# Last LayerNorm and output store moved into the block of the last experts, with the statistics taken on transposed sums

## The reference

```python
def _layernorm(x, axis=-1, eps=1e-05):
    m = jnp.mean(x, axis=axis, keepdims=True)
    v = jnp.var(x, axis=axis, keepdims=True)
    return (x - m) / jnp.sqrt(v + eps)

# ... seven such lines before it
x = _layernorm(x + _L3_ffn_ref(x, ...), axis=-1)     # L3_ffn: 8 routed experts (top 2) and a shared one
return x                                              # (4, 512, 128), float32
```

## Time and profile before

| | us |
|---|---|
| median of 3 runs | 1772.24 (1771.27 to 1776.8) |
| the profiled execution, own time | 1770.54 |
| its span, first to last instruction | 1768.4 |
| PE busy in it | 1613.3 (91%) |
| DVE / ACT / POOL busy | 1049.9 / 1012.7 / 746.8 |

### The profile page before, as it was taken

How to read it: one execution, slowest core, us unless ns; L and a number is a source line. 1 busy time by engine, 2 the same in 40 slices (tenths; PEclk the granted TensorE clock), 3 DMA queues, 4 the chain that set the end, 5 groups by cost and what they waited for, 6 DMA issues and landing times. The chain is left out here.

```text
span 1768.4 us, 28482 instructions
## 1 busy us (share of the span) xinstructions
PE 1613.3 (91%) x9207; PEld 1084.4 (61%) x9225; DVE 1049.9 (59%) x2605; ACT 1012.7 (57%) x2188; POOL 746.8 (42%) x683
## 2 busy tenths in 40 slices
PE   5888998888798899999799999999999999888998
PEld 3556754346596677777555555555458886344786
DVE  5865775623122666666366666666558886662675
ACT  4534563553243555555466666666548887754786
POOL 1234533105252566655265555555234443021463
PEclk8999998998899999999999999999989999989999
DMA  1008323000214223232211111111046562000420
GB/s 43 2 15 179 69 73 142 1 1 30 68 34 138 60 65 68 61 69 51 78 44 47 47 40 47 47 39 49 19 144 218 219 221 87 1 1 22 148 108 25
DMA packets 61868, 124.71 MB, mean 71 GB/s; under 512 B 14258, under 2 KB 29477, under 8 KB 55228
## 3 DMA queue, kind: packets, MB, share of 16 engines
q1 hardware_dynamic: 59580, 119.24, 23.1%
q0 software_dynamic: 2144, 3.70, 0.7%
HBM read 79.05 MB, written 11.02 MB: 51 GB/s over the span
## 5 line engine op out<-in xcount | busy, mean ns | idle before, releaser
L1992 ACT ACTIVATE h_probs<-psum,h_nmax 128x512 f32<-128x512 f32 (+3 forms) x256 | 133.2, 526 | 119.0 <-DVE h_nmax L2073 64.1
L2073 DVE CUSTOM_DVE_ANT_0 psum<-psum,h_mask 128x512 f32<-128x512 f32 (+3 forms) x256 | 122.6, 511 | 83.3 <-PE psum L1876 80.4
L917 ACT ACTIVATE psum<-psum,f_b 128x512 f32<-128x512 f32 x200 | 132.3, 662 | 30.0 <-PE psum L874 30.0
L1804 POOL TENSOR_TENSOR h_swapped<-h_swapped,rope_tables 128x512 f32<-128x512 f32 x64 | 81.8, 1278 | 153.6 <-DMA h_swapped<-h_raw 153.6
L840 POOL TENSOR_TENSOR e_lo<-e_gated,e_hi 128x512 fp32r<-128x512 f32 x59 | 76.0, 1289 | 150.3 <-ACT e_hi L929 150.3
L2425 ACT ACTIVATE a_probs<-psum,a_nmax 128x512 f32<-128x512 f32 (+3 forms) x128 | 67.5, 527 | 120.7 <-DVE a_nmax L2500 70.3
L2246 POOL TENSOR_TENSOR a_swapped<-a_swapped,a2f_a_tables 128x512 f32<-128x512 f32 x64 | 82.0, 1281 | 127.1 <-DMA a_swapped<-a_raw 127.0
L952 DVE TENSOR_TENSOR e_lo<-psum,e_hi 128x512 fp32r<-128x512 f32 x168 | 114.8, 683 | 24.9 <-ACT psum L917 24.9
L126 PE MATMUL psum<-rope_tables,mean_w 128*128 128x256 f32 x482 | 118.3, 396 | 7.0 <-ACT h_raw L1982 2.8
L1883 PEld LDWEIGHTS psum<-ident,h_probs 128*128 128x128 f32 x640 | 71.4, 141 | 80.4 <-issue 52.8
L1883 PE MATMUL psum<-ident,h_probs 128*128 128x128 f32 x640 | 115.1, 287 | 1.7 <-ACT h_probs L1992 1.4
(11 more groups left out here) (501 smaller groups left out, 4135.7 us busy)
## 6 DMA issues: line engine op xcount, KB each, us to landing
e_gate<-gates SPq DMA_DIRECT2D x39, 1024.0 KB, 4.7
a_swapped<-a_raw SPq DMA_DIRECT2D x128, 128.0 KB, 2.3
h_swapped<-h_raw SPq DMA_DIRECT2D x256, 64.0 KB, 2.0
e_gate<-gates SPq DMA_DIRECT2D x16, 512.0 KB, 8.0
f_w<-in_l_experts SPq DMA_DIRECT2D x32, 128.0 KB, 4.6
slots<-a_empty SPq DMA_DIRECT2D x1, 2600.0 KB
f_w<-in_l_experts SPq DMA_DIRECT2D x9, 256.0 KB, 4.9
e_got<-slots SPq DMA_DIRECT2D x7, 325.0 KB, 4.2
```

The costliest lines, as they stand in the source:

```text
L917: nc.scalar.activation(to, hidden_bank(n), ex.act_func, **bias(n)).then_inc(act_ready, 1)
L1992: nc.scalar.activation(probs[:, j % 4, 0:(q + 1) * P], ring[j % RING][:, 0:(q + 1) * P], ACT.Exp, scale=-1.0, bias=nmax[:, j % 8:j % 8 + 1 ...
L2073: nc.vector.tensor_tensor_reduce(s, s, mask[:, (QT - 1 - q) * P:], scale=-1.0, scalar=-SENT, op0=ALU.add, op1=ALU.min, accum_out=nmax[:, j ...
```

## The change

`store_end` and its block are gone. A new class `StoreTail` hands each engine a piece of program that runs at the end of its program in the block of the last experts. PE turns the raw sums (`sum_fm`) instead of normed values, into PSUM banks 0 to 3, each block as soon as `added` allows it, and `keep_busy` at this place goes. With tokens on partitions, mean and variance of a token are a matter of its own row: DVE takes them by BN_STATS (6 numbers for each tile of 128 tokens) and BN_AGGR (2 numbers), ACT makes the inverse root on 128x4 numbers (Ln, Exp). The norm itself is one instruction for each 128x128 tile, from PSUM into the tile to be stored: blocks 0 and 2 on DVE (subtract mean, multiply), blocks 1 and 3 on ACT (Identity with a scale and a bias for each partition; the bias, -mean * inverse, comes from DVE as `tail_shift`). The four stores keep their shape.

```diff
--- before.py
+++ after.py
@@ -349,46 +349,79 @@
                 head.vector(dve)
 
 
-class StoreFront(Ahead):
+class StoreTail:
 
 
     def __init__(self, core, st):
-        self.core = core
+        self.core, self.nc = core, core.nc
         self.out = core.dram["out"].rearrange("(t p) c -> p t c", p=P)
         self.xt = st.sb("x_tm", [P, NT, P])
-        self.tiles_ready, self.tiles_out, self.stored = (st.sem(n) for n in ("tiles_ready", "tiles_out", "stored"))
-
-    def tensor(self, pe, out_ready):
-        nc, core = self.core.nc, self.core
+        self.stats = st.sb("tail_stats", [P, NT, 6])
+        self.mean_var = st.sb("tail_mean_var", [P, NT, 2])
+        self.inverse, self.shift = (st.sb(f"tail_{n}", [P, NT]) for n in ("inverse", "shift"))
+        self.tiles_ready, self.measured, self.gathered, self.log_ready, self.inverse_ready, self.shift_ready, self.stored = (
+            st.sem(f"tail_{n}") for n in ("tiles_ready", "measured", "gathered", "log_ready", "inverse_ready", "shift_ready", "stored"))
+        self.tiles_out = [st.sem(f"tail_{n}_out") for n in ("even", "odd")]
+
+    def tensor(self, pe, added, count):
         for b in range(B):
-            pe.wait_ge(out_ready, b + 1)
-            if b >= 2:
-                pe.wait_ge(self.tiles_out, b - 1)
-            for q in range(QT):
-                last = nc.tensor.transpose(core.psum[:, b % 2, q * P:(q + 1) * P], core.x[:, (b * QT + q) * P:(b * QT + q + 1) * P], core.ident[:])
+            pe.wait_ge(added, count + b + 1)
+            for t in range(b * QT, (b + 1) * QT):
+                last = self.nc.tensor.transpose(self.core.psum[:, b, t % QT * P:(t % QT + 1) * P], self.core.sum[:, t * P:(t + 1) * P], self.core.ident[:])
             last.then_inc(self.tiles_ready, 1)
 
-    def copy(self, dve, b):
-        dve.wait_ge(self.tiles_ready, b + 1)
-        self.core.nc.vector.tensor_copy(self.xt[:, b * QT:(b + 1) * QT, :].rearrange("p t c -> p (t c)"), self.core.psum[:, b % 2, :]).then_inc(self.tiles_out, 1)
-
-    def vector(self, dve, b):
-        if b >= 1:
-            self.copy(dve, b - 1)
-        if b == B - 1:
-            self.copy(dve, b)
+    def scalar(self, act):
+        nc = self.nc
+        nc.scalar.preload_act_table_set("natural_log_exp_and_others")
+        for b in range(B):
+            of = slice(b * QT, (b + 1) * QT)
+            act.wait_ge(self.gathered, b + 1)
+            nc.scalar.activation(self.inverse[:, of], self.mean_var[:, of, 1], ACT.Ln, bias=self.core.eps[:, 0:1]).then_inc(self.log_ready, 1)
+            act.wait_ge(self.log_ready, b + 1)
+            nc.scalar.activation(self.inverse[:, of], self.inverse[:, of], ACT.Exp, scale=-0.5).then_inc(self.inverse_ready, 1)
+            if b % 2 == 1:
+                act.wait_ge(self.shift_ready, b // 2 + 1)
+                for t in range(b * QT, (b + 1) * QT):
+                    last = nc.scalar.activation(self.xt[:, t, :], self.core.psum[:, b, t % QT * P:(t % QT + 1) * P], ACT.Identity,
+                                                scale=self.inverse[:, t:t + 1], bias=self.shift[:, t:t + 1])
+                last.then_inc(self.tiles_out[1], 1)
+
+    def vector(self, dve):
+        nc = self.nc
+
+        def moments(b):
+            dve.wait_ge(self.tiles_ready, b + 1)
+            for t in range(b * QT, (b + 1) * QT):
+                last = nc.vector.bn_stats(self.stats[:, t, :], self.core.psum[:, b, t % QT * P:(t % QT + 1) * P])
+            last.then_inc(self.measured, 1)
+            dve.wait_ge(self.measured, b + 1)
+            for t in range(b * QT, (b + 1) * QT):
+                last = nc.vector.bn_aggr(self.mean_var[:, t, :], self.stats[:, t, :])
+            last.then_inc(self.gathered, 1)
+
+        def finish(b):
+            dve.wait_ge(self.inverse_ready, b + 1)
+            of = slice(b * QT, (b + 1) * QT)
+            if b % 2 == 1:
+                dve.wait_ge(self.gathered, b + 1)
+                nc.vector.scalar_tensor_tensor(self.shift[:, of], self.mean_var[:, of, 0], -1.0, self.inverse[:, of], ALU.mult, ALU.mult).then_inc(self.shift_ready, 1)
+            else:
+                for t in range(b * QT, (b + 1) * QT):
+                    last = nc.vector.tensor_scalar(self.xt[:, t, :], self.core.psum[:, b, t % QT * P:(t % QT + 1) * P], self.mean_var[:, t, 0:1],
+                                                   self.inverse[:, t:t + 1], ALU.subtract, ALU.mult)
+                last.then_inc(self.tiles_out[0], 1)
+
+        moments(0)
+        for b in range(1, B):
+            moments(b)
+            finish(b - 1)
+        finish(B - 1)
 
     def sync(self, sp):
         for b in range(B):
-            sp.wait_ge(self.tiles_out, b + 1)
+            sp.wait_ge(self.tiles_out[b % 2], b // 2 + 1)
             sp.dma_start(self.out[:, b * QT:(b + 1) * QT, :], self.xt[:, b * QT:(b + 1) * QT, :]).then_inc(self.stored, 16)
         sp.wait_ge(self.stored, 16 * B)
-
-
-def store_end(core):
-
-    with Stage(core, "store") as st:
-        norm(core, "n3f", core.sum, core.x, StoreFront(core, st))
 
 
 class WindowFront(Ahead):
@@ -732,7 +765,7 @@
                                                skip_group_check=True)
 
 
-def experts(core, name, ex):
+def experts(core, name, ex, tail=None):
 
 
 
@@ -816,6 +849,8 @@
                         sp.dma_start(gate[rows, s % ring, :], row.partition_broadcast(P // up)).then_inc(gate_loaded[s % ring], 16)
                     if s + ring - 1 < n_slots:
                         ex.load_weights(sp, s + ring - 1)
+                if tail is not None:
+                    tail.sync(sp)
 
             @block.gpsimd
             def _(pool):
@@ -899,7 +934,10 @@
                     if n + ahead < n_items:
                         hidden(n + ahead)
                     output(n)
-                keep_busy(core, pe, 0, 3)
+                if tail is not None:
+                    tail.tensor(pe, added, (n_slots - 1) * B)
+                else:
+                    keep_busy(core, pe, 0, 3)
 
             @block.scalar
             def _(act):
@@ -932,6 +970,8 @@
                     for n in range(n_items):
                         activate_rounded(n)
                         activate(n)
+                    if tail is not None:
+                        tail.scalar(act)
                 else:
                     activate(0)
                     for n in range(n_items):
@@ -983,6 +1023,8 @@
                             low_part(n)
                         if n >= 2 and (n - 2) % tiles == tiles - 1:
                             gate_pair((n - 2) // tiles)
+                    if tail is not None:
+                        tail.vector(dve)
                 else:
                     gate_item(0)
                     for n in range(n_items):
@@ -1697,7 +1739,7 @@
                             hid_bias_dram=d["l3_gb1"], more_loads=[(b1[:], d["l3_b1"]), (b2[:], d["l3_b2"])])
         head = Head(core, layer_norm(core, st, "n3a"), ahead=front)
         router(core, "r3", "softmax_top", front, head, top=2, gates_t=gt, ex=ex)
-        experts(core, "e3", ex)
+        experts(core, "e3", ex, StoreTail(core, st))
 
 
 def rope_attention(core, name, front, head, *, x, heads):
@@ -3437,7 +3479,6 @@
         ffn2(core)
         hawk(core)
         ffn3(core)
-        store_end(core)
 
 
 def arrays(i):
```

## The result

| | median us | ratio to before, 95% interval |
|---|---|---|
| before | 1772.40 (9 executions, 1771.27 to 1783.17) | |
| after | 1764.09 (9 executions, 1759.63 to 1768.26) | 0.9947 (0.9924 to 0.9971) |

I had said 1768.0 and a range from 1765.8. The span of the profiled execution is 1766.4 us and its own time 1768.21, so it is one of the longer of the nine.

What follows compares the result with a forecast made beforehand. A latency-bound tail, with no engine full for the last 15.00 us, bounds the kernel. Summed DVE and ACT steps end at 1761.37, plus 2.75 gives 1764.12, 4.3 us less: 1772.24 - 4.3 = 1768.0, range 1765.8 to 1771.2.

Steps and rivals of the forecast that it cites:

- a block of moments in DVE's stream: In the tail: one block's four BN_STATS and four BN_AGGR take 1.33 us of DVE, lower end 1.20, upper 2.24.
- DVE's wait for ACT ahead of norm 2: In the tail: DVE waits some 0.7 us for ACT's inverse of block 2 before norming that block.
- from there to the end: From the last tile ready to the end of the span, issuing and landing the last store: 2.75 us, kept unchanged.
- my lower end: In the tail's moments: a BN_STATS priced as a plain 128x128 copy from PSUM, 0.28 us long, four in 0.88.
- The hole behind ACT's norm of block 1: In the tail: ACT's Ln for block 2 stands behind that norm, leaving DVE nothing to do from 1757.89; norm 2 starts 1758.59.
- the first line of the sum: Start of the tail: DVE begins the moments at 1751.36, 0.08 us before its last gate multiply ends.
- My part on what goes: Around the tail: barrier, block entry, hidden table load, PE's centering and averaging, wide ACT and DVE instructions and `keep_busy` go.
- Rival 1: In the tail: nothing overlaps on DVE and ACT in these small forms; gain 1.2 us, time 1771.0, chance 0.13.
- Rival 2: In the tail: statistics cheaper than the copy, or block end costs less than kept; gain over 5.3 us, 1766.5, chance 0.25.
- Rivals 3 and 4: In the tail: statistics run several passes, 1778.8 us, chance 0.04; POOL's last add holds the norm back, given nothing.

Runs made afterwards that it cites:

- t_best: The changed kernel with another tail order: DVE takes moments of all blocks before any norm, ACT norms blocks 0 and 2; ratio 0.9960 to before, tail 11.53 us.
- c_alloc: The kernel before with five unused tiles of the new tail's shapes allocated ahead of the last experts' own; ratio 0.9973 to before.
- d_late: The changed kernel with the tail's five tiles allocated behind the last experts' own instead of ahead of them; ratio 0.9973 to before.
- r_before: The kernel before, unchanged, run again; median 1771.25 us of 12, ratio 0.9989 to before.
- p_512: The kernel before with 512 unused bytes a partition ahead of the last experts' tiles, executed once for the profile; upstream 1664.38 us, matmul starts 232.2 ns apart.
- p_384: The kernel before with 384 unused bytes ahead of the last experts' tiles, executed once for the profile; upstream 1666.96 us, matmul starts 226.7 ns apart.

## Why the prediction was wrong

Its terms, by their measured size:

| step | predicted | measured |
|---|---|---|
| DVE's first statistics behind the last expert matmul | 0.71 | 0.71 |
| four BN_STATS | 0.93 | 0.86 to 0.89 (0.282 each) |
| four BN_AGGR | 0.44 | 0.38 (0.157 each) |
| a block of moments in DVE's stream | 1.33 | 1.21 |
| DVE norm of a block | 1.12 | 1.34, 1.36 (0.401 each) |
| ACT norm of a block | 1.53 | 1.50 |
| DVE's wait for ACT ahead of norm 2 | 0.7 | 0.78 |
| last tile behind the last expert matmul | 10.72 | 10.67 |
| from there to the end | 2.75 | 2.74 |
| tail, gain | 4.3 | 4.37 |
| experts' stage, gain | 0 | 2.29 |
| outside the span, gain | 0 | 0.31 |

The groups of instructions after, with the mean length of one, which answer to the borrowed rows:

```profile
L395 DVE BATCH_NORM_STATS2 f_tail_stats<-psum 128x6 f32<-128x128 f32 x16 | 3.5, 282 | 0.0
L385 ACT ACTIVATE f_x_tm<-psum,f_tail_shift,f_tail_inverse 128x128 f32<-128x128 f32 x8 | 3.0, 456 | 3.1 <-DVE f_tail_shift L407 3.1
L410 DVE TENSOR_SCALAR f_x_tm<-psum,f_tail_mean_var,f_tail_inverse 128x128 f32<-128x128 f32 x8 | 2.7, 401 | 0.8 <-ACT f_tail_inverse L381 0.8
...
L399 DVE BATCH_NORM_AGGREGATE f_tail_mean_var<-f_tail_stats 128x2 f32<-128x6 f32 x16 | 1.5, 157 | 0.1
```

**The tail was right**, mechanism and size, with two errors that cancel, which is luck: the three blocks of moments on the path are 0.12 us cheaper each than I took (a statistic costs what a copy does, my lower end), 0.36 together, and the two norms on DVE 0.22 and 0.24 dearer, 0.46 together, since the TENSOR_SCALAR with two pointers is 0.401 long against the 0.344 of the instruction with one that I borrowed. I had that length only as an upper end. Whether the second pointer or the other form costs the 0.06, no run separates. The hole behind ACT's norm of block 1 was there, and t_best closed it.

**What failed is the first line of the sum**: "DVE starts at 1751.36", that is, all ahead of the tail stays as it was. I put what happens in the experts' stage at nothing, without a reason. My part on what goes listed instructions and waits, but the change also allocates 8.8 KB a partition ahead of two tiles that TensorE reads in half of the 432 matmuls of that stage, and with the old placement matmuls of every kind there were slower. 2.3 us, with 0.3 outside the span, make 4.37 + 2.29 + 0.31 = 7.0 of the gain, 0.9961 of 1772.4, inside both measured intervals (0.9924 to 0.9971 and 0.9937 to 0.9987). Forecast with these, the time would have been 1765.4. The 1764.09 of the first nine lie 1.3 below that, within the scatter of upstream.

**The range was too narrow by the same scatter.** Eighteen profiles of one upstream program run from 1648.66 to 1666.96 us. I took 0.5 us of scatter, though my three times already lay 5.5 apart; a median of nine of such executions moves by more.

**Rival 1** (nothing overlaps) is refuted: four BN_STATS of 0.282 in 0.88 start 0.20 apart. Nor does TENSOR_SCALAR wait for the one before it (0.401 long, four in 1.34, so 0.31 apart). I had read only half of the section of the Trainium skill that I cited for this rival ("VectorE: DVE Perf Modes", "The DRAIN you can't avoid"): it goes on that "A next op that is not held starts earlier". The rows agree with that half. **Rival 2** had the right sign and a chance of 0.25, but named the end of the block and cheaper instructions; that its time came nearer was mostly luck. The end of the block gave 0.3 outside the span. The last store had not been queueing (2.74 against 2.75). My argument for it misread the stores of before as 1.2 us apart: they go out at 1762.44, 1763.64, 1764.83 and 1765.67, so the last only 0.84 behind the third, and even that did not hold it up. **Rivals 3 and 4** did not occur: BN_STATS took 0.282 us, and PE was ready for block 3 at 1756.23 where DVE came to it at 1758.63.

## What to carry to other kernels

A tile allocated ahead of others is part of a change: before calling the rest of a kernel untouched, compare the addresses, and if a stage's matmul spacing moves with the same instructions, undo the allocation alone (c_alloc, d_late) before explaining it by the code. For a latency-bound tail a sum over borrowed start-to-start distances came out within 0.1 us of 10.7, here with two errors of about 0.4 us that cancelled, and such a sum also shows which engine waits behind another's order. And three times do not give the scatter: look at the granted clock by window, and compare stretches of the profile instead of totals when the effect is a few microseconds.

## What the runs showed of the hardware that I had not expected

- Matmuls of 512 columns of rounded fp32, with TensorE full at clock 1.00, start 226.7 ns apart or 231.7 to 232.2 ns, by whether the moving tiles `e_hi` and `e_lo` stand at the same offset modulo 256 bytes of the partition as `f_x_hi` and the weights (18 profiles, no exception; of unequal offsets only 128 and 192 were run). The mechanism is open.
- BN_STATS of 128 columns of fp32 from PSUM is 0.282 us long and starts every 0.20; BN_AGGR of one tile is 0.157.
- The same upstream instructions take up to 18 us more or less. In the window from 1283 to 1300 the granted clock was 0.84 and 0.80 in r_before and before, 0.60 in both profiles of after and in c_alloc. The two longest upstreams, p_512 (first) and p_384, already have a clock of 0.70 from 255 to 300, where before (third) has 0.81:

```profile
255.00:300.00 45.00, 40.03 (x234) 23.68 (x238) 23.77 (x46) 8.13 (x12) 17.15 (x18) 0.70 0.53 200
```

```profile
255.00:300.00 45.00, 38.26 (x215) 23.67 (x219) 24.28 (x44) 7.13 (x10) 19.57 (x19) 0.70 0.54 203
```

```profile
255.00:300.00 45.00, 37.84 (x272) 20.68 (x275) 27.92 (x56) 12.10 (x19) 18.69 (x19) 0.81 0.53 200
```

They had done 234 and 215 matmuls in it against 272. TensorE was not idle more there (40.0 and 38.3 us busy against 37.8), so the level of the clock is what differs: one stretch of 27.3 us at 1.2 GHz in both against 17.1 in before, and both are 7.1 us later behind it, measured against before from 250 to 302. What sets the level from one execution to the next I did not find.
